# Where the turned mask is added: VectorE instead of TensorE at eleven of 32 steps instead of five

## The reference, cut to what matters

```python
# layer 0, for each of 16 graphs, 8 heads of 32
q, k, v = x @ Wq.T + bq, x @ Wk.T + bk, x @ Wv.T + bv
scores = q @ k.T / sqrt(32)                    # 8 x 512 x 512
scores = where(adj + eye > 0, scores, -inf)    # the mask, the same for all heads
attn = softmax(scores); out = attn @ v
h = layernorm(x + out @ Wo.T + bo) * gamma + beta
# layer 1, one head with logits of rank two
feat = h @ fc_w.T + fc_b
logits = (feat @ q_w.T + q_b) + (feat @ k_w.T + k_b).T + (1 - adj) * -1e9
y = softmax(leaky_relu(logits)) @ feat + h
```

## Time and profile before

| what | value |
|---|---|
| median of 3 runs | 1097.93 us (1094.98 to 1108.29) |
| the profiled execution's own time | 1106.9 us |
| its span | 1104.8 us |
| mean granted TensorE clock | 0.971 |
| TensorE busy | 92% |
| VectorE busy | 71% |
| GpSimd busy | 65% |
| ScalarE busy | 56% |

### The profile page before, as it was taken

One profiled execution on the slowest core, in us unless ns is written; L12 is line 12 of the kernel. 1 busy time (PEld: TensorE's weight loads), 2 busy tenths in 40 slices (PEclk: granted clock), 3 DMA queues, 4 the chain that ended last, 5 costly groups with the idle time before them and its releaser, 6 DMA issues. The chain is left out here.

```text
span 1104.8 us, 16668 instructions
## 1 busy us (share of the span) xinstructions
PE 1021.8 (92%) x5720; PEld 649.2 (59%) x5720; DVE 782.6 (71%) x1945; ACT 622.8 (56%) x1180; POOL 722.8 (65%) x415
## 2 busy tenths in 40 slices
PE   5789899999999999999999998999999999999866
PEld 4445565656656565665666564666656566665454
DVE  4667777877767787777778777777767767775432
ACT  2145466565646557575655657564555746566633
POOL 3056787675667667666777766576766657778740
PEclk9899999999999999999999999999989999999978
DMA  5677827576564667667374767646366663745010
GB/s 133 106 123 145 133 73 143 102 144 96 113 116 89 135 113 144 96 121 127 102 134 83 153 115 137 103 103 119 79 141 105 136 108 99 135 76 90 29 48 28
DMA packets 81571, 120.89 MB, mean 109 GB/s; under 512 B 9296, under 2 KB 36432, under 8 KB 81488
## 3 DMA queue, kind: packets, MB, share of 16 engines
q1 hardware_dynamic: 81488, 119.84, 56.8%
HBM read 52.44 MB, written 8.39 MB: 55 GB/s over the span
## 5 line engine op out<-in xcount | busy, mean ns | idle before, releaser
L708 ACT ACTIVATE e<-st_bank 128x512 f32<-128x512 f32 x512 | 307.4, 602 | 404.1 <-PE st_bank L526 223.5
L928 DVE CUSTOM_DVE_ANT_0 sm_bank<-sm_bank,masks 128x512 f32<-128x512 f32 x512 | 354.1, 693 | 155.3 <-PE sm_bank L534 152.2
L1009 POOL TENSOR_TENSOR e_sum<-e_sum,e 128x1024 f32<-128x1024 f32 x128 | 303.7, 2385 | 49.8 <-ACT e L708 49.8
L534 PE MATMUL sm_bank<-kt_hi,q_pad 128*128 128x512 f32 x512 | 281.9, 552 | 32.9 <-issue 28.0
L524 PE MATMUL st_bank<-q_stack,k_stack 97*128 97x512 f32 x432 | 197.7, 458 | 3.8 <-ACT e L708 3.0
L1009 POOL TENSOR_TENSOR e_sum<-e 128x1024 f32<-128x1024 f32 x64 | 152.2, 2378 | 67.9 <-ACT e L708 61.1
L526 PE MATMUL st_bank<-mask_t,ident_b 128*128 128x512 bf16 x432 | 169.2, 392 | 0.0
L524 PEld LDWEIGHTS st_bank<-q_stack,k_stack 97*128 97x128 f32 x432 | 81.5, 189 | 111.5 <-ACT e L708 103.3
L462 PE MATMUL o_bank<-e,v 128*32 128x512 f32 x1024 | 136.4, 605 | 0.7 <-ACT e L708 0.7
L505 PE MATMUL shared<-feat,z 128*128 128x256 f32 x512 | 134.5, 412 | 1.4 <-ACT z L651 1.4
L534 PEld LDWEIGHTS sm_bank<-kt_hi,q_pad 128*128 128x128 f32 x512 | 103.2, 202 | 44.5 <-issue 31.8
(11 more groups left out here) (131 smaller groups left out, 1836.7 us busy)
## 6 DMA issues: line engine op xcount, KB each, us to landing
adj_in<-in_adj SPq DMA_DIRECT2D x32, 1024.0 KB, 7.8
q_stack<-qt_hi SPq DMA_DIRECT2D x64, 256.0 KB, 9.7
k_stack<-kt_hi SPq DMA_DIRECT2D x64, 256.0 KB, 8.8
x_in<-in_x SPq DMA_DIRECT2D x16, 512.0 KB, 10.4
q_pad<-qt_hi SPq DMA_DIRECT2D x128, 64.0 KB, 7.7
q_stack<-qt_lo SPq DMA_DIRECT2D x32, 256.0 KB, 8.6
k_stack<-kt_lo SPq DMA_DIRECT2D x32, 256.0 KB, 11.9
h<-in_x SPq DMA_DIRECT2D x16, 512.0 KB, 3.8
```

The lines of the kernel that those rows point to most:

```text
L534: nc.tensor.matmul(sm_bank[s % 2][:, :], q_pad[j // GH][:, j % GH, qt * P:(qt + 1) * P], kt_hi[j // GH][:, :], start=True, stop=True).then ...
L708: nc.scalar.activation(e[:, kt, i, :], st_bank[s % 2][:, :], ACT.Exp, scale=SCALE)\
L928: nc.vector.tensor_tensor_reduce(sm_bank[s % 2][:, :], sm_bank[s % 2][:, :], mask[nxt if off else par][:, qt * N:(qt + 1) * N], 1.0, LOWES ...
L1009: nc.gpsimd.tensor_tensor(e_sum[:, pair, :], a, b, ALU.add).then_inc(pool_done.sem, 1)
```

## The change

The list of steps at which VectorE adds the turned mask grows from five to eleven: steps 5, 6, 16, 17, 27 and 31 are new. At each of them TensorE issues one matmul (and its weight load) less, VectorE issues one add of 128 by 512 more, ahead of that step's maximum, and ScalarE's exponential waits for VectorE instead of TensorE. The scores part runs in 16 iterations, so 96 matmuls go and 96 adds come. No transfer is added or removed.

```diff
@@ -42,7 +42,7 @@
 EPS = 1e-5
 LOWEST = -3.0e38
 STACK = 3 * DH
-DVE_MASKED = (12, 14, 15, 26, 29)
+DVE_MASKED = (5, 6, 12, 14, 15, 16, 17, 26, 27, 29, 31)
 LEAD = 21
 
 FIRST, LAST = -1, NB + 1
```

## The result

The changed kernel takes 1112.2 us (median of 15 runs), the kernel before 1101.56 us in the same comparison: ratio 1.0097, 95% interval 1.006 to 1.0134. The forecast was +12.7 us on 1097.93, a ratio of 1.0116. The profiled execution took 1118.6 us, its span is 1116.6 us. Executions of one kernel scatter by some 20 us (the changed one: 1107.5 to 1128.0), and a profile shows one of them: that of the kernel before, 1106.9 us at a granted clock of 0.971, is slower than its medians of 1094.4 to 1101.6 us in the comparisons of this document.

A forecast was written before the change was run, and what follows sets the result against it. The loop was taken as set by the q_pad0 landing behind queued stack copies, and by TensorE and VectorE up to l_max3. 0.35 + 0.56 = 0.91 us on 14 iterations, 12.7 us, took 1097.93 to 1110.6 us; range 1097 to 1124.

The forecast's parts named there:

- What bounds the kernel: Loop: the q_pad0 landing behind queued copies sets sm(11), 18.20 us from l_max3; TensorE and VectorE carry the other 44.10 us.
- A matmul is worth 0.23 us, an add costs 0.60: Any listed step: a removed mask matmul saves TensorE 0.23 us; an inserted add holds VectorE 0.60 us.
- Steps 31, 5, 6: matmuls worth 0, cover enough: Between l_max3 and sm(11): three matmuls (0.69 us) gain 0; q_hi0 1.65 us late, hidden by 4.3 us of copy queue.
- the cover went: Adds at 5 and 6 no longer hidden before sm(11): each iteration would then pay the rest of the delay.
- Steps 16 and 17: +0.35 us: Two adds delay max(18) and so sm(20): +0.55 us instead of -0.46, less 0.2 absorbed, +0.35 us an iteration.
- the part given back: Turn of h at step 22, already waiting for ScalarE, absorbs 0.2 us of the delay at sm(20).
- Step 27: 0: TensorE gains 0.23 us but waits it before the key logits, held by step 28's query logits: 0.
- Step 31: +0.56 us: Add between l_max1 and l_max3 on VectorE, without idle time: l_max3, transfers and sm(11) 0.56 us later an iteration.
- Sum: 0.91 us, 12.7 us in all: 0.35 + 0.56 us on each of 14 iterations; first iteration and tail 0, within 3 us either way.
- The clock unchanged: After sm(11): as many half-clock iterations as before (six of 13 windows, about 1.6 us each), since idle time there rather shrinks.
- Rival C: Wait at step 8 halves the clock in all 14 iterations, or GpSimd's chain slips: 13 us more, 1124 us; chance 0.17.
- The Trainium skill's rules: Relieving the busiest engine first would give 1075.8 us, though its busy share is a poor measure; idleness brings the slow clock.

The follow-up runs named there:

- the fastest kernel: Kernel before with the last two stack copies behind the q_pad0 copies, then step 24 added, then o_lo1 ahead of l_mask on GpSimd: 1065.4 us, ratio 0.9715.

## Why the prediction was right, and where it was not

- **What bounds the kernel.** Right. sm(11) follows the landing by 0.09 us in 13 of 13 iterations of the kernel before and in 12 of 13 of the changed one, the landing follows `l_max3` and the backlog, and moving the copies ahead of a third of the backlog gave 2.1%, where 32 matmuls fewer (steps 5 and 6) gave nothing.
- **A matmul is worth 0.23 us, an add costs 0.60.** Right in both; the adds stand 0.6 us apart from what follows.
- **Steps 31, 5, 6: matmuls worth 0, cover enough.** Right in the usual iteration: `q_hi0`'s copies left 1.4 us later (1.65 forecast) and the landing stayed. Where the adjacency landed 11.4 us (once in the changed kernel) or 12.6 us (once with steps 5 and 6 alone) behind its issue, the cover went, the copies landed 3.0 and 3.8 us before sm(11), and TensorE, held at step 7 for 4.0 and 4.4 us, set it. The forecast names that case but puts it at nothing.
- **Steps 16 and 17: +0.35 us.** The mechanism is right, the size a little off: +0.26 us alone. sm(20) came 0.51 us later against st(16), where 0.55 was forecast, so the rest of the error is in the part given back: 0.25 instead of 0.2 us.
- **Step 27: 0.** It was -0.12 us. The wait for the query logits takes half, not all. With steps 16 and 17 it makes +0.14; the changed kernel has +0.16.
- **Step 31: +0.56 us.** 0.55 measured.
- **Sum: 0.91 us, 12.7 us in all.** 0.71 us measured, 9.9 us, with 10.6 us in the medians. The profiled execution came within 1 us of its forecast (1118.6 against 1119.6), and that is luck: 3.8 us of the difference lie ahead of the first sm(11) and 2.7 us behind the last, where the forecast had 0 within 3 us, and the periods between give 5.4 us and not 12.
- **The clock unchanged.** About right for the whole change. In one execution each, 6 and 4 slow stretches stand at sm(11), and two of the changed kernel's stand ahead of it, so that in both TensorE spent 27.3 us of the 13 periods at 1.2 GHz. But the reason given, that the idle time at sm(11) shrinks, leaves out that its parts pull apart: step 31 alone lowered the clock (0.966 against 0.980), and with steps 5 and 6 beside it the clock was that of the kernel before (0.975). Rival C's 13 us did not come. It took the wait at step 8 for an addition to TensorE's idle time; beside step 31 it is a piece cut out of the wait at sm(11) (2.18 us in all against 2.19).
- **The Trainium skill's rules.** Relieving the engine with the largest busy share would have meant TensorE, and 96 matmuls fewer brought nothing. The Trainium skill ("Perfetto Trace Analysis", Identifying the Most-Contended Engine) has the most-contended engine optimized first, but judges TensorE's headroom by its useful work or its weight loads and not by its matmuls' busy share. Weight loads are busy 59% here, less than VectorE's 71%, so by that measure it does not speak for this change. On the clock, the Trainium skill ("TensorE: Matmul & The Clock Gate", What's actually happening) ties the slow clock to idleness. The runs agree, and the same idle time in two pieces was followed by it less often (8 of 13 iterations against 3 of 13, one execution each).

Left open: how the 1.5% of step 31 alone divides between the loop and the clock. The loop's piece makes 0.7% and leaves 0.8%. But over the 29 runs of the kernel before in that comparison a clock lower by 0.001 goes with 1.0 us more, and by that slope the 0.014 between the two kernels would be some 15 of the 17 us, and the loop's 7.7 us would hardly be seen. Also open is whether the last two steps of the fastest kernel gain anything each.

## What to carry to other kernels

A wait that returns once in every iteration and that no instruction releases is the first thing to explain, however busy the busiest engine is: follow it from the landing back to the issue and to what stands ahead in the queue. Work taken from an engine counts only between two points of the loop where that engine is what comes last, and work given to another costs where it stands ahead of a result that is waited for; the same add cost 1.5% in front of `l_max3` (about half of it through the loop, the rest probably through the clock) and nothing behind it. Before moving work between engines, look at the order on the queue that feeds the wait.

## What the runs showed of the hardware

TensorE's clock fell behind waits much shorter than an iteration. Where the idle time before sm(11) was 2.17 us in the mean and in one piece, the 1.2 GHz level followed in 8 of 13 iterations; at 1.23 us there, with 0.74 us waited at steps 8 and 9, in 3 of 13; at 0.27 us, with the rest at step 0, in none. The total from `l_max3` to sm(11) was nearly the same in the three (2.19, 2.18 and 1.99 us). These are counts of one execution each, and no rule for the single wait: in the kernel before, the level fell behind waits of 1.63 to 2.74 us and did not behind one of 3.05 us. In the slow stretch eight matmuls took 2.98 us instead of 1.89. A delay of 0.55 us an iteration (0.7%) thereby went with 1.5% more time. The adjacency's transfer of 1 MB usually landed some 7 us after its issue, and once in an execution it could take 11.4 us (the changed kernel, sm(11) 22.6 us behind `l_max3`), 12.5 us (steps 16 and 17 alone, 22.0 us) or 12.6 us (steps 5 and 6 alone, 24.5 us); in these three the period was 2.8 to 5.4 us longer than the mean. What makes it late no run shows.

Small copies wait behind large ones of the same queue: those of 64 KB took 6.1 us to land with six copies of 256 KB issued ahead of them, 3.7 us with four, and 1.9 us where they were issued so late that little was left ahead.
